# Graph attention in one kernel of four layers: row term as a bias of ScalarE's copies, shorter score product, later division

## The reference, cut to what matters

```python
def gat_layer(x, adj, W, a_self, a_neigh, b):
    feat = jnp.einsum('nf,hfo->hno', x, W)                 # 8 heads of 32
    attn_self = jnp.einsum('hno,ho->hn', feat, a_self)
    attn_neigh = jnp.einsum('hno,ho->hn', feat, a_neigh)
    e = attn_self[:, :, None] + attn_neigh[:, None, :]     # row term + column term
    e = jax.nn.leaky_relu(e, LRELU_ALPHA)                  # 0.2
    e = e + MASK_VAL * (1.0 - adj)[None, :, :]
    alpha = jax.nn.softmax(e, axis=-1)
    out = jnp.einsum('hnm,hmo->hno', alpha, feat) + b[:, None, :]
    out = jnp.transpose(out, (1, 0, 2)).reshape(out.shape[1], -1)
    return jax.nn.elu(out)
```

## Time and profile before

| what | us |
|---|---|
| median of three timed runs | 1138.37 |
| lowest, highest | 1137.56, 1141.92 |
| the profiled execution, its own time | 1142.99 |
| its span in the trace | 1141.2 |
| mean granted clock of TensorE in it | 0.943 |

### The profile page before, as it was taken

The page is one execution under the profiler, slowest core; times in us unless marked ns, Lnnn a source line. Parts: engine busy times, 40 slices in busy tenths (PEclk is TensorE's granted clock), DMA queues, the critical chain, the costliest instruction groups (busy, mean ns, idle before and its releaser), DMA issues.

```text
span 1141.2 us, 20328 instructions
## 1 busy us (share of the span) xinstructions
PE 1045.9 (92%) x6046; PEld 851.3 (75%) x6046; DVE 847.6 (74%) x2613; ACT 605.4 (53%) x1686; POOL 415.2 (36%) x358
## 2 busy tenths in 40 slices
PE   5999988399999458999999999999998999999997
PEld 3556565246666247899999999999987888888886
DVE  6878687427775478977777777777777888888887
ACT  3578585243333238777777777777864222222221
POOL 4688686360000433332333333322322232323321
PEclk9999697569999769999999999999999999999999
DMA  8900000311111221101011010000010111111111
GB/s 251 373 15 1 1 2 1 104 56 45 43 47 47 69 98 38 47 1 38 6 43 38 1 34 1 2 1 2 2 42 15 43 42 55 41 55 41 45 52 37
DMA packets 55459, 53.46 MB, mean 47 GB/s; under 512 B 5536, under 2 KB 48864, under 8 KB 55376
## 3 DMA queue, kind: packets, MB, share of 16 engines
q1 hardware_dynamic: 52560, 46.87, 13.0%
q0 software_dynamic: 1536, 4.20, 1.1%
q10 hardware_dynamic: 1280, 1.38, 0.5%
HBM read 43.25 MB, written 9.18 MB: 46 GB/s over the span
## 4 chain that ended last, share of the span: by engine, by line
PE 75%; POOL 8%; DVE 7%; issue 4%; ACT 4%; DMA 2%; another core or an unknown queue 0%; ACTq 0%; DVEq 0%; POOLq 0%
PE bank L57 13%; PE bank L58 13%; PE bank L59 13%; PE bank L921 7%; PE bank L942 5%; PE bank L818 4%; PE bank L843 4%; PE bank L826 3%; PE bank L931 3%; POOL rest L1362 3%; PE bank L943 2%; POOL alpha L1365 2%; PE bank L616 1%; PE bank L900 1%; POOL g_pos L1340 1%
## 5 line engine op out<-in xcount | busy, mean ns | idle before, releaser
L1435 POOL TENSOR_TENSOR rot_s<-swap,rq 128x512 f32<-128x512 f32 x64 | 88.4, 1382 | 198.5 <-ACT swap L1214 198.5
L1090 ACT ACTIVATE silu<-bank 128x512 f32<-128x512 f32 x66 | 39.5, 599 | 173.5 <-PE bank L59 173.5
L1962 DVE TENSOR_TENSOR o_ring<-bank,o_ring 128x256 fp32r<-128x256 f32 x128 | 54.3, 424 | 83.8 <-ACT o_ring L1243 83.0
L1227 ACT ACTIVATE prob<-prob,pmin 128x128 f32<-128x128 f32 (+1 forms) x256 | 113.2, 446 | 2.8 <-DVE pmin L1943 2.8
L921 PE MATMUL bank<-kv,norm 128*128 128x128 f32 (+1 forms) x512 | 106.5, 331 | 6.2 <-DVE norm L1936 6.1
L1784 DVE SCALAR_TENSOR_TENSOR xs<-bank,wt,xs 128x256 f32<-128x256 f32 x264 | 109.0, 475 | 0.1
L1383 POOL TENSOR_TENSOR gate_r<-gate_w,gate_r 128x256 fp32r<-128x256 f32 x31 | 36.4, 1175 | 177.2 <-ACT gate_r L1083 177.2
L1243 ACT ACTIVATE o_ring<-bank 128x256 fp32r<-128x256 f32 x128 | 48.4, 378 | 80.1 <-PE bank L943 79.9
L57 PE MATMUL bank<-wo_r,o_ring 128*128 128x256 f32 x256 | 84.1, 328 | 0.0
L1943 DVE CUSTOM_DVE_ANT_0 prob<-bank,causal 128x128 f32<-128x128 f32 (+1 forms) x256 | 80.1, 350 | 0.3 <-PE bank L921 0.2
L1955 DVE TENSOR_SCALAR prob<-prob,pinv 128x128 f32<-128x128 f32 (+1 forms) x256 | 75.9, 339 | 4.6
(11 more groups left out here) (287 smaller groups left out, 3119.0 us busy)
## 6 DMA issues: line engine op xcount, KB each, us to landing
gate_w<-in_Wg SPq DMA_DIRECT2D x33, 128.0 KB, 2.1
up_w<-in_Wu SPq DMA_DIRECT2D x33, 128.0 KB, 2.2
down_w<-in_Wd SPq DMA_DIRECT2D x33, 128.0 KB, 2.2
w_all<-in_w_gate SPq DMA_DIRECT2D x8, 512.0 KB, 10.2
w_all<-in_w_up SPq DMA_DIRECT2D x8, 512.0 KB, 10.4
w_all<-in_w_down SPq DMA_DIRECT2D x8, 512.0 KB, 10.5
wq_g<-in_Wq SPq DMA_DIRECT2D x4, 1024.0 KB, 5.6
wo_g<-in_Wo SPq DMA_DIRECT2D x4, 1024.0 KB, 5.5
```

The source lines that it names most:

```text
L1227: ins = act.activation(prob[:, u % 4, nt * P:nt * P + (nt + 1) * P], prob[:, u % 4, nt * P:nt * P + (nt + 1) * P], ACT.Exp, bias=pmin[:, u ...
L1435: pool.tensor_tensor(rot_s[:, m % 2].rearrange("p (b n) -> p b n", b=2), swap[:, m % 2].rearrange("p (b n) -> p b n", b=2), bcast(tab[:, 1 ...
```

## The change

Four edits.

1. The row term no longer goes through TensorE for each unit. `self_columns(r)` on TensorE makes, once a round, the row terms of all eight heads as columns (two products of 8 columns), VectorE's `keep_columns(r)` copies them to `s_col` (times 1 or 0.2 by head), and ScalarE adds the column as the bias of the copy out of PSUM. That copy becomes two instructions of 128x256 (one for each row tile, since the bias differs), with the function Identity in place of Copy. `edges(k)` is left with one product of 256 columns, since both row tiles read the same column term. The array `ind` shrinks from 48x1152 to 48x16 numbers.
2. `divide(j)` stands one step later, `exp_out(j)`, `positive(j)` and `elu(j)` two steps later, and with them `turn_x1`, `add_x1`, the measurement of the rows and the last rounds' tables. The loop has 77 steps in place of 75; the added ones carry no unit.
3. The last of each 16 turned units is copied by VectorE (L1558 before) and no longer by ScalarE: 32 copies each, before 36 by ScalarE and 28 by VectorE.
4. The product with noughts is gone: the first product of a bank carries the start flag instead.

Also VectorE does `keep_columns(0)` and `neighbours(0)` before `measure(1)`.

```diff
         def copied_by_dve(k):
-            return k % 2 == 1 and k % 16 != 15
+            return k % 2 == 1
...
+                def self_columns(r):
+
+                    if r == 0:
+                        pe.wait_ge(S["ind_done"], 1)
+                    else:
+                        pe.wait_ge(S["col_copied"], r)
+                    pe.wait_ge(S["st_copied"], 2 * r + 2)
+                    for nt in range(NT):
+                        mm = pe.matmul(MISC[:, N + nt * GH:N + nt * GH + GH], st_parts[:, r % 2, nt * P:nt * P + P],
+                                       ind[:, :, 1], start=True, stop=True)
+                    mm.then_inc(S["col_ready"], 1)
...
-                    if h == 0:
-                        pe.wait_ge(S["st_copied"], 2 * r + 2)
                     if k >= 2:
                         pe.wait_ge(S["z_copied"], k - 1)
-                    pe.matmul(ZB[k % 2].rearrange("p (u n) -> p u n", u=NT), ind[:, h, 0:P],
-                              bcast(st_parts[:, r % 2, :], 1, NT), start=True, stop=False)
-                    for nt in range(NT):
-                        mm = pe.matmul(ZB[k % 2][:, nt * N:nt * N + N].rearrange("p (u n) -> p u n", n=PAD),
-                                       st_parts[:, r % 2, nt * P:nt * P + P],
-                                       bcast(ind[:, h, P:], 1, N // PAD), start=False, stop=nt == NT - 1)
-                    mm.then_inc(S["z_ready"], 1)
+                    pe.matmul(ZB[k % 2][:, 0:N], ind[:, h, 0:1].to_broadcast([TR, P]), st_parts[:, r % 2, :],
+                              start=True, stop=True
+                              ).then_inc(S["z_ready"], 1)
...
+                    if (r := starts_in(k, 3)) is not None:
+                        self_columns(r)
...
-                    if r == 0:
-                        pe.wait_ge(S["nought_set"], 1)
-                        pe.matmul(W_BANK[b2][:], nought[:, 0:P], nought[:], start=True, stop=False)
...
-                    act.activation(alpha[:, k % RING, :], ZB[k % 2][:], ACT.Copy, scale=NEG if k % 2 else 1.0).then_inc(S["z_copied"], 1)
+                    r, h = divmod(k, UNITS)
+                    if h == 0:
+                        act.wait_ge(S["col_copied"], r + 1)
+                    for nt in range(NT):
+                        ins = act.activation(alpha[:, k % RING, nt * N:nt * N + N], ZB[k % 2][:, 0:N], ACT.Identity,
+                                             bias=s_col[:, r % 2, nt, h:h + 1], scale=NEG if k % 2 else 1.0)
+                    ins.then_inc(S["z_copied"], 1)
...
-                    if (j := quad_at(k, 1)) is not None:
+                    if (j := quad_at(k, 3)) is not None:
                         exp_out(j)
...
-                if (j := quad_at(k, 1)) is not None:
+                if (j := quad_at(k, 3)) is not None:
                     positive(j)
...
+                def keep_columns(r):
+
+                    dve.wait_ge(S["col_ready"], r + 1)
+                    if r >= 2:
+                        dve.wait_ge(S["z_copied"], UNITS * (r - 1))
+                    dve.tensor_tensor(s_col[:, r % 2].rearrange("p u h -> p (u h)"), MISC[:, N:N + NT * GH],
+                                      s_scale[:].rearrange("p u a j -> p (u a j)"), ALU.mult).then_inc(S["col_copied"], 1)
...
-                    if (j := quad_at(k, 1)) is not None:
+                    if (j := quad_at(k, 2)) is not None:
                         divide(j)
-                    if (j := quad_at(k, 2)) is not None:
+                    if (j := quad_at(k, 4)) is not None:
                         elu(j)
```

More of the change, by code:

```diff
@@ L33 @@
 QUAD = 4
-PAD = 16
 RING = 6
@@ L189, in build @@
         wst1 = sb_early("wst1", [P, HC, TR])
-        ind = sb_early("ind", [TR, GH, P + PAD], F32R)
+        ind = sb_early("ind", [TR, GH, 2], F32R)
         st_parts = sb_early("st_parts", [TR, 2, N], F32R)
@@ L193, in build @@
         neg_rstd = sb_early("neg_rstd", [P, T])
+        sb_early("spare", [P, 1120])
+        s_col = sb_early("s_col", [P, 2, NT, GH])
+        s_scale = sb_early("s_scale", [P, NT, GH // 2, 2])
         row_sum = sb_early("row_sum", [P, 2, NT, QUAD])
@@ L335, in build @@
         ALLQ = ROUNDS * QUADS
-        LAST = ALL + 11
-        NORM_AT, TURN_AT, ROUTE_AT = (ALL, ALL + 2, ALL + 8), (ALL + 2, ALL + 4, ALL + 9), (ALL + 4, ALL + 6, ALL + 10)
+        LAST = ALL + 13
+        NORM_AT, TURN_AT, ROUTE_AT = (ALL, ALL + 2, ALL + 10), (ALL + 2, ALL + 4, ALL + 11), (ALL + 4, ALL + 6, ALL + 12)
         def starts_in(k, lead):
@@ L681, in graph_attention @@
                     features(0, nt)
+                self_columns(0)
                 for k in range(-1, LAST):
@@ L693, in graph_attention @@
                         weigh(j)
-                    if (r := round_at(k, 17)) is not None:
+                    if (r := round_at(k, 19)) is not None:
                         turn_x1(r)
@@ L961, in project_out @@
                             [o_ring[:, u % O_RING, j, nt * P:nt * P + P] for j in range(2)],
-                            [wo_r[:, g % 2, j, r, :] for j in range(2)], False, r == REP - 1 and nt == NT - 1)
+                            [wo_r[:, g % 2, j, r, :] for j in range(2)], r == 0 and nt == 0, r == REP - 1 and nt == NT - 1)
                     mm.then_inc(S["o_used"], 1)
@@ L1370, in _ @@
                     inverse(k // 2)
-                if (r := round_at(k, 20)) is not None:
+                if (r := round_at(k, 22)) is not None:
                     inverse(r)
@@ L1476, in prepare_vectors @@
             def prepare_vectors():
+                dve.memset(s_scale[:, :, :, 1:2], NEG)
+                dve.memset(s_scale[:, :, :, 0:1], 1.0)
                 chain.link(dve.memset(wst0[:], 0.0))
@@ L1598, in graph_attention @@
                 prep(0)
+                keep_columns(0)
+                neighbours(0)
                 measure(1)
-                neighbours(0)
                 for k in range(LAST):
@@ L1617, in graph_attention @@
                         prep(r)
+                    if (r := starts_in(k, 3)) is not None:
+                        keep_columns(r)
                     if (j := quad_at(k, -2)) is not None:
                         invert(j)
-                    if (j := quad_at(k, 1)) is not None:
+                    if (j := quad_at(k, 2)) is not None:
                         divide(j)
-                    if (j := quad_at(k, 2)) is not None:
+                    if (j := quad_at(k, 4)) is not None:
                         elu(j)
-                    if (r := round_at(k, 18)) is not None:
+                    if (r := round_at(k, 20)) is not None:
                         add_x1(r)
-                    if (r := round_at(k, 19)) is not None:
+                    if (r := round_at(k, 21)) is not None:
                         measure(r)
@@ L2051 @@
     before[:, P:] = np.arange(TILES, dtype=np.float32)
-    ind = np.zeros((TR, GH, P + PAD), np.float32)
+    ind = np.zeros((TR, GH, 2), np.float32)
     for h in range(GH):
-        ind[[h, ROW + h], h, :P] = -1.0
-        ind[[GH + h, ROW + GH + h], h, P:] = -1.0
+        ind[[h, ROW + h], h, 0] = -1.0
+        ind[[GH + h, ROW + GH + h], h, 1] = -1.0
     arrays = dict(
```

10 lines of the change are left out of this document (3 added, 7 removed).

## The result

The changed kernel takes 1130.78 us in the median of five runs (1129.93 to 1131.52) against 1138.37 of the kernel before in the same comparison (1136.08 to 1142.23). The ratio is 0.9923, with a 95% interval of 0.9903 to 0.9943: 7.6 us less. The forecast was 1120, 18.4 us less, so the sign was right, the time inside the stated range, and the gain 2.4 times too large. In a later comparison the same kernel came to 0.9930 (0.9905 to 0.9954).

What follows compares the result with a forecast made beforehand. TensorE was taken to bound causal attention and early graph-attention quads, GpSimd later ones. Terms -6, -1.5, +0.5, -8, +1, -1.5 and -3.4 sum to -18.9 from 1138.4, rounded to 1120 us; range 1110 to 1134.

Steps and rivals of the forecast that it cites:

- The base: Whole kernel: profiled execution 1142.99 us, median 4.6 lower, so the gain of 18.9 was taken off 1138.4.
- Quads, 9.2 at full clock and 9.8 late: Graph attention: three quads from 69 to 98 us at 9.2 each, -1.5; eight from 98 to 185 at 9.8, -8.
- Noughts, -3.4: Causal attention, where TensorE bounds: 16 products with noughts of 0.21 us each removed, -3.4 us.
- Start, -1.5: From 14 to 43 us: a few shorter score products, between 0 and -3 us, taken as -1.5.
- One score product at 0.40: TensorE at 1.2 GHz: one 256-column product at 0.40 us saves 0.75 a unit; two early quads -6.
- End and added waits, +0.5 and +1: Graph attention: two unit-less steps at the end cost +0.5 us; waits around self_columns and keep_columns +1.
- Copy with a bias: ScalarE: two copies at 0.80 us replace one of 0.48, 1.3 us more a quad, making its load 9.0.
- A: Rival, chance 0.15: TensorE's clock stays at the lower level from 69 to 208 us; 1133 us.
- B: Rival, chance 0.14: no clock dips that matter, 11 quads at 9.0 us; 1111 us.
- C: Rival, chance 0.08: the division wait only changes its place; only score products and noughts pay; 1125 us.
- D: Rival, chance 0.05: single score product costs 0.72 us, lower clock throughout; slower, about +12.5, 1151 us.
- E: Rival, chance 0.08: ScalarE bounds with two copies of 0.50 us, 11 quads at 10.0; about +5, 1125 us.

Runs made afterwards that it cites:

- f1: The changed kernel timed and profiled once more with no edit; median 1130.34 us, ratio 0.9930 to the kernel before.
- e1: The kernel before, timed and profiled once more with no edit; median 1137.78 us, ratio 0.9976.
- e4: The kernel before with only the product with noughts taken away; median 1137.35 us, ratio 0.9966.
- f4: The kernel before with the product with noughts issued twice; median 1140.54 us, ratio 1.0033.
- f3: The changed kernel with VectorE's copy of the turned unit moved ahead of its step's mask additions; median 1124.51 us, ratio 0.9875.
- k2: The changed kernel with VectorE's copy first, plus the old lags for the last two quads and last round, 75 steps; median 1125.68 us, ratio 0.9901.
- k4: The changed kernel with two plain copies instead of copies with a bias, row term left out; median 1128.34 us, ratio 0.9927.
- e2: The kernel before with only the row term as bias and one score product a unit; median 1136.28 us, ratio 0.9972.
- e3: The kernel before with only the later division (one step) and elu (two steps); median 1134.22 us, ratio 0.9953.
- f2: The changed kernel with three unused products of 256 columns ahead of each unit's score product; median 1140.04 us, ratio 1.0013.

## Why the prediction was right or wrong

**The sign and the places were right, the size was not: two steps of the likeliest case failed.** The first is the base: a sum worked out on a long execution was taken off the median. The second is the term for the quads, 9.2 us at full clock and 9.8 late: the division's wait went, but GpSimd and ScalarE did not run into their own sums; they ran into a wait of TensorE for VectorE, and a quad took 10.0. The noughts come third.

Set beside each other, the two profiled executions (1142.99 and 1130.78 us) close the account:

| part, by landmarks | forecast | measured |
|---|---|---|
| to quad 0 | -1.5 | -3.2 |
| quad 0 to 2 | -6 | -6.7 |
| quad 2 to 13 (-1.5, -8, and +1 for added waits) | -8.5 | -5.3 |
| quad 13 to the similarity product | +0.5 | +3.4 |
| from there on, the noughts in it | -3.4 | -0.4 |
| sum of these | -18.9 | -12.2 |
| the profiled execution of before above its median | 0 | +4.6 |
| against the median | -18.9 | -7.6 |

A pair of single traces is not more exact than 1 or 2 us: with f1's trace the fourth row is +0.8.

- *The base, 4.6 us.* The profiled execution was one in which TensorE came late to its full clock, and I subtracted a gain that exists only there from the median of all. Against before and e1 the first two quads gain 6.7 (25.7 to 19.06), as worked out; against e4 and f4, the same code, they gain 0.9. The changed kernel came early to the full clock in both its traces, and its profiled execution was the median one. I had seen the 4.6 us and kept them as a constant offset; they were part of the same time that the change saves, and so counted twice. This is the largest single error.
- *Quads, 9.2 at full clock and 9.8 late.* For quads 3 to 13 these figures make 96.8 us. The changed kernel took 99.6 and 100.2, before 105.7. The step that failed is the sentence "It takes the waits of rows 3 away", with GpSimd and ScalarE then in their own sums of 8.63 and 9.0. The waits went, but I never asked what GpSimd, now running on, would meet. It met VectorE's mask addition, nine times instead of three, with TensorE's next input queued behind. f3, which lets that input go first, brings the ten quads to 95.2. The error is about 3 us.
- *Noughts, -3.4.* -1.6 to -1.8. The price of 0.21 us was right in the steady blocks; that nothing else would move was not, and the first block gave 1.0 us back.
- *Start, -1.5.* Quad 0's products begin at 36.3 and 37.5, in the four traces of the old stage at 38.4 to 39.6: -2.0 on the mean, of the right size.
- *One score product at 0.40.* The chain has 0.51 for L611 at the lower clock (115.15): 0.64 saved a unit, not 0.75. Its bounds held.
- *End and added waits, +0.5 and +1.* k2 finds nothing for the end. `self_columns` and `keep_columns` show in none of the larger waits of the changed kernel.
- *Copy with a bias.* Priced at +0.32 a unit. In the timeline two copies start at 111.18 and the next instruction at 111.89, 0.71 for the pair where 0.80 was taken, and k4 shows that even this is mostly off the path.

Whether the edits add up the medians can't say: e2, e3 and e4 are 1.5, 3.6 and 0.4 us below e1, 5.5 together, and 12.3 together below the kernel before of their comparison; the whole change is 7.6 and 7.2.

**The rivals.** A: no, by f2; the granted clock from 98 to 185 us was 0.81 and 0.79. B: no; the full-clock period is 9.0 to 9.1 where nothing collides, but there are long quads in every round. C: no, the division's waits are gone. D: its price of about 0.5 came (0.51), its other condition, the lower clock throughout, did not. E: no, by k4; its sum was also wrong, since three quads at +0.8 and eight at +0.2 are +4 and not +5. What came in was no rival of mine: a wait of another pair of engines, made by the wait that went.

What stays open: what decides when TensorE gets its full clock in a given execution, and how much of f3's gain is the meeting of the two additions and how much the plain order. f3 doesn't take the dips away (0.84 from 69 to 185 us).

## What to carry to other kernels

When a change takes a wait away, ask of each engine that is let go what it will be doing at that moment, and which other engine shares something with it; then look what is queued behind the one that loses. An instruction that only hands data on (here the copy of a turned unit) belongs ahead of longer work of the same step if the next engine is idle without it.

When the profiled execution differs from the median by as much as the expected gain, find out in which stage the difference lies before subtracting. If it is the stage that the change rewrites, the gain has to be worked out for both kinds of execution.

When a saving repeats in every block, compare the blocks one by one. The six steady blocks gave the forecast price of the noughts to 0.01 us; the total hid it behind one block that had moved the other way.

## What the runs showed of the hardware

- A VectorE addition with two inputs in SBUF that starts while GpSimd is in an addition of the same kind ends 0.28 us after it, in all nine cases over 1.1 us of the changed kernel: 1.48 us in place of 0.41 in most of them. Beside GpSimd's one-input instructions it took at most 0.82 us, in 55 of 69 cases at most 0.43.
- Identical code got the full TensorE clock at 41.0 and 42.7 us in two executions and at 67.3 and 68.2 in two others; that alone makes 20.0 or 25.7 us of the same two quads. The window view gives 1.00 before the clock's first record, whatever the level is.
- Three filler products of 256 columns a unit did not raise the granted clock from 69 to 185 us (0.82 against 0.79 and 0.81) and cost 9.7 us for 192 products. The seven traces with the short product came to the full clock at 38.2 to 42.0 us, the seven with the full columns at 41.0 to 68.2.
- A copy from PSUM with a bias, 128x256, takes 0.36 us of ScalarE in a row of two, a plain one 0.26 (k4); an ordinary copy of 128x512 takes 0.48.
